# A macaron layer on eight cores: loads of the combine stage issued three tiles ahead, and the output projection's loads on two queues

## The chip, the cores and the metric

One Trainium2 chip, all 8 cores. Each core computes one of the 8 batch entries (2048 tokens x 1024 features, float32) with the same program, and no data passes between cores. The metric is the device time of the slowest core in microseconds.

## The reference, cut to what matters

The layer is half a feed-forward block, attention, and half a feed-forward block again, each on a layer norm of its input. In the feed-forward block every group of 32 tokens is dispatched: each of 128 experts (32 experts x 4 sets) takes the one token of the group with the largest logit, works on it, and its result is added back to that token.

```python
def _L0_ffn_ref(x, controller, f1, bias, f2):
    grouped = x.reshape(B, g, t, d)                      # t = 32
    logits = jnp.einsum('bgtd,des->bgtes', grouped, controller)
    logits = logits + tie
    perm = (logits == jnp.max(logits, axis=-3, keepdims=True))
    dispatched = jnp.einsum('bgtd,bgtes->bgesd', grouped, perm)
    inner = relu(jnp.einsum('bgesd,desf->bgesf', dispatched, f1) + bias)
    intermediate = jnp.einsum('bgesf,esfd->bgesd', inner, f2)
    return jnp.einsum('bgesd,bgtes->bgtd', intermediate, perm)

x = x + 0.5 * _L0_ffn_ref(_layernorm(x), ...)
x = x + _L0_attn_ref(_layernorm(x), ...)   # 16 heads, relative positions, projection by Wo
x = x + 0.5 * _L0_ffn_ref(_layernorm(x), ...)
```

## The kernel before, in words

There is no scheduler. A small builder (class `Bld`) collects one list of instructions for each engine: PE (`tensor`), DVE (`vector`), ACT (`scalar`), POOL (`gpsimd`, GpSimd) and SP (`sync`). Each engine works through its list in order. `b.wait(engine, semaphore, value)` puts a wait into a list, and everything behind it on that engine waits too. `b.dma` (L61) issues a transfer from SP's or GpSimd's list; SP and GpSimd have a DMA queue each (in the profile q1, hardware_dynamic, and q0, software_dynamic), and both are served by the same 16 DMA engines. All SBUF buffers are stretches of one tensor `SCR`, so the profile calls nearly every tile `SCR`.

The program runs in stages, one behind the other:

1. `emit_ln` (layer norm of 2048 tokens), then `emit_ffn`: permutation matrices (L290 to L339), dispatch (L451 to L482), the experts (L519, L575, L605). The result of the experts goes to HBM, to `itb`, in 128 KB pieces by GpSimd.
2. The **combine stage** at the end of `emit_ffn`, L650 to L726. It goes over 16 tiles `t` of 128 tokens. For each, `load_rhs` (L658) loads 4 pieces of `itb`, each 128 x 1024 floats, 512 KB, two from SP and two from GpSimd; `load_xt` (L673) loads the residual tile of `x` or `xs`, 512 KB, from SP. PE multiplies with the permutation (8 matmuls of 128x128x512 at L700; each float32 matmul stands in the trace as two records, so 16 per tile), DVE does `0.5 * P1 + x` in one instruction (L713), and SP stores the tile (L722, 512 KB). PE may not write `P1` again before DVE has read it (L696). There are two buffers for `itb` (`RHS2` and 4096 columns behind it) and two for the residual (`XT`), used in turn.
3. `emit_ln`, then `emit_attn`: 8 pairs of heads, 32 iterations each. Then the **output projection**, L1049 to L1113: eight loads of `aofm` (the attention's result, 1 MB each) and eight of `wot` (512 KB each), then 16 tiles with 16 matmuls of 128x128x512 (L1081) and two additions on DVE (L1093, L1101).
4. `emit_ln` and `emit_ffn` again, with a second combine stage. Its stores go to `out` and end the program.

SP's list in the combine stage is what sets its order. Before the loads of tile t+1 stand these two waits, for PE's work on tile t-1 (which read the `itb` buffer that is filled next) and for the store of tile t-1 (which reads the residual buffer that is filled next):

```python
                    if t >= 1:
                        b.wait("sync", "pe", pesc_hist[t - 1])
                        b.wait("sync", "so", st_hist[t - 1])
                        b.wait("gpsimd", "pe", pesc_hist[t - 1])
                    pre_rhs.append(load_rhs(t + 1, (t + 1) % 2))
                    pre_xt.append(load_xt(t + 1, (t + 1) % 2))
```

`barrier(eng)` (L117) makes one engine wait for everything that was issued so far, by one wait for each semaphore. It stands ahead of each layer norm and ahead of the projection's loads. `DS` (8192 columns from `HBASE + 8192`) holds the dispatched tokens for the experts; in the combine stage nothing reads it.

Of the kernel before, what the change touches and what calls it, by code (L numbers as in the profile page):

```python
# [16 lines left out]
NT = 16  # L17
# [47 lines left out]
def build_nc():  # L65
# [24 lines left out]
    aofm = nc.dram_tensor("aofm", [DM, S], F32).ap()  # L90
# [4 lines left out]
    with ExitStack() as stack:  # L95
        SCR = stack.enter_context(nc.sbuf_tensor("SCR", [128, SCRW], F32))
# [7 lines left out]
        b = Bld(nc, stack)  # L104
        for s_ in ("ld", "sx", "so", "fla", "flb", "fba", "fbb", "fbc", "fbd",
                   "gm", "qwa", "qwb", "qwc", "gra", "grb", "grc",
                   "iwa", "iwb", "rha", "rhb", "xta", "xtb", "aow",
                   "hw", "hr", "lxa", "lxb", "lxc", "lxd", "rga", "rgb",
                   "pe", "ac", "ve"):
            b.sem(s_)  # L110
        DMA_SEMS = ("ld", "sx", "so", "fla", "flb", "fba", "fbb", "fbc", "fbd",
                    "qwa", "qwb", "qwc",
                    "gra", "grb", "grc", "iwa", "iwb", "rha", "rhb",
                    "xta", "xtb", "aow", "hw", "hr", "lxa", "lxb", "lxc", "lxd",
                    "rga", "rgb")

        def barrier(eng):  # L117
            for s_ in DMA_SEMS + ("gm", "pe", "ac", "ve"):
                b.wait(eng, s_, b.cnt[s_])

        def scr(lo, hi, p0=0, p1=128):
            return SCR[p0:p1, lo:hi]
# [140 lines left out]
        def emit_ffn(src_hbm, dst_hbm, h_ve):  # L263
# [11 lines left out]
            DS = HBASE + 8192  # L275
            RHS2 = TAIL
# [9 lines left out]
            for t in range(NT):  # L286
                b.wait("tensor", "ve", b.cnt["ve"])
                for m in range(8):
                    b.op("tensor",
                         lambda e, t=t, m=m: e.matmul(  # L290
                             P1[:, 128 * m:128 * (m + 1)],
                             scr(HBASE + 1024 * t + 128 * m,
                                 HBASE + 1024 * t + 128 * (m + 1)),
                             IDENT[:, :], start=True, stop=True,
                             is_transpose=True),
# [143 lines left out]
            for gh in range(2):  # L439
                for grp in range(2):  # L440
                    for ti in range(8):
                        t = 8 * gh + ti
# [212 lines left out]
            b.wait("gpsimd", "ve", b.cnt["ve"])  # L655
            b.wait("tensor", "ve", b.cnt["ve"])

            def load_rhs(t, slot):  # L658
                lasts = [0, 0]
                for a in range(4):  # L660
                    g = 4 * t + a
                    src = AP(itb.tensor, g * DM, [[NG * DM, 128], [1, DM]])
                    eng = "sync" if a % 2 == 0 else "gpsimd"
                    sem = ("rha" if slot == 0 else "rhb") if a % 2 == 0 \
                        else ("rga" if slot == 0 else "rgb")
                    lasts[a % 2] = b.dma(eng,
                                         SCR[:, RHS2 + 4096 * slot + 1024 * a:
                                             RHS2 + 4096 * slot
                                             + 1024 * (a + 1)],
                                         src, sem)  # L670
                return lasts

            def load_xt(t, slot):  # L673
# [2 lines left out]
                             src_hbm[128 * t:128 * (t + 1), :],  # L676
                             "xta" if slot == 0 else "xtb")

            pre_rhs = [load_rhs(0, 0)]
            pre_xt = [load_xt(0, 0)]  # L680
            pesc_hist = [0] * NT
            vres_hist = [0] * NT
            st_hist = [0] * NT
            st_last = None
            for t in range(NT):
                if t + 1 < NT:
                    if t >= 1:
                        b.wait("sync", "pe", pesc_hist[t - 1])
                        b.wait("sync", "so", st_hist[t - 1])
                        b.wait("gpsimd", "pe", pesc_hist[t - 1])  # L690
                    pre_rhs.append(load_rhs(t + 1, (t + 1) % 2))
                    pre_xt.append(load_xt(t + 1, (t + 1) % 2))
                b.wait("tensor", "rha" if t % 2 == 0 else "rhb", pre_rhs[t][0])
                b.wait("tensor", "rga" if t % 2 == 0 else "rgb", pre_rhs[t][1])
                if t >= 1:
                    b.wait("tensor", "ve", vres_hist[t - 1])  # L696
                for bk in range(2):
                    for a in range(4):
                        b.op("tensor",
                             lambda e, t=t, a=a, bk=bk: e.matmul(  # L700
                                 P1[:, 512 * bk:512 * (bk + 1)],
                                 scr(PRMP + 512 * t + 128 * a,
                                     PRMP + 512 * t + 128 * (a + 1)),
                                 SCR[:, RHS2 + 4096 * (t % 2) + 1024 * a + 512 * bk:
                                     RHS2 + 4096 * (t % 2) + 1024 * a
                                     + 512 * (bk + 1)],
                                 start=(a == 0), stop=(a == 3)),
                             inc="pe")
# [19 lines left out]
        def emit_attn(src_hbm, dst_hbm, hfm_ve):  # L728
# [320 lines left out]
            AOF = XA  # L1049
            XTO = HBASE + 8192  # L1050
            barrier("sync")
            ldw = None
            for m in range(8):
                b.dma("sync", SCR[:, AOF + 2048 * m:AOF + 2048 * (m + 1)],
                      aofm[128 * m:128 * (m + 1), :], "sx")
            for m in range(8):
                ldw = b.dma("sync",
                            SCR[:, HBASE + 1024 * m:HBASE + 1024 * (m + 1)],
                            wot[128 * m:128 * (m + 1), :], "sx")
            b.wait("tensor", "sx", ldw)  # L1060
            b.wait("tensor", "ac", b.cnt["ac"])
            st_last = None
            xt_pre = [b.dma("sync", SCR[:, XTO:XTO + 1024],
# [157 lines left out]
```

How the kernel before makes its waits and increments, by code:

```python
    def wait(self, eng, semname, val):  # L45
        if val is None or val <= 0:
            return
        s = self.sems[semname]
        self.th[eng].append(lambda e, s=s, v=val: e.wait_ge(s, v))
# [1 line left out]
    def op(self, eng, fn, inc=None, n=1):  # L51
        if inc is None:
            self.th[eng].append(fn)
            return None
        self.cnt[inc] += n
        s = self.sems[inc]
        self.th[eng].append(lambda e, fn=fn, s=s, n=n: fn(e).then_inc(s, n))
        return self.cnt[inc]
```

## Time and profile before

| What | Value |
|---|---|
| two timed runs | 9095.19 and 9497.57 us, median 9296.38 us |
| the profiled execution | 8977.86 us |
| its span, from the first to the last instruction of the slowest core | 8975.5 us (the 8 cores: 8934.5 to 8975.5 us) |
| busy share: PE, DVE, ACT, POOL | 86%, 20%, 19%, 6% |
| mean granted clock of PE, as a share of full speed | 0.870 to 0.873 on the 8 cores |
| first combine stage | 1486.2 to 1717.7 us |
| output projection, from its first load to its last tile | 6945.7 to 7288.6 us |
| second combine stage | 8751.5 us to the end |

The times of the profile are microseconds from the start of the span of core 2, the slowest. PE is the matmul engine, PEld its weight loads, SPq the issuing of transfers by SP. "Idle before, releaser" is how long an engine stood still before an instruction and what ended that. The DMA share is the mean busy share of the core's 16 DMA engines; GB/s is what they moved.

### The profile page before, as it was taken

How to read it: one execution, taken by the hardware profiler on the slowest of the kernel's cores; microseconds unless marked ns; L12 is line 12 of the kernel's file. 1: busy time of each engine (PE TensorE's matmuls, PEld its weight loads, DVE VectorE, ACT ScalarE, POOL GpSimd, SP SyncE). 2: the span in 40 equal slices, each digit the busy share in tenths (PEclk: the TensorE clock that was granted, in tenths of full speed). 3: DMA queues.
4: the chain of work that ended last, by engine and by line, in shares of the span. 5: the costliest groups of instructions: out<-in, count | busy, mean ns of one | idle time of the engine just before them, and what ended most of it. 6: DMA issues, size and time to landing. Idle time of an engine off the chain costs nothing.

```text
span 8975.5 us, 109129 instructions; the slowest of 8 cores (8934.5 to 8975.5 us)
## 1 busy us (share of the span) xinstructions
PE 7715.6 (86%) x44416; PEld 5238.7 (58%) x44416; DVE 1750.6 (20%) x3535; ACT 1706.7 (19%) x1511; POOL 573.8 (6%) x1096
## 2 busy tenths in 40 slices
PE   3888887489899899899999999899998757888885
PEld 3664563247757657567577577477477336456542
DVE  3221120202202212112112122022022133112110
ACT  0112212002212212112122122122122000221220
POOL 0001101000000000000000000000000000110110
PEclk7678769789999999999999999999899875986788
DMA  2124325514314324224134144044143220431336
GB/s 81 55 60 133 83 56 167 187 41 153 136 57 155 110 78 158 87 103 157 63 126 155 41 147 158 32 157 143 46 153 135 96 87 0 115 106 54 88 107 225
DMA packets 342583, 962.91 MB, mean 107 GB/s; under 512 B 38096, under 2 KB 198096, under 8 KB 275280
## 3 DMA queue, kind: packets, MB, share of 16 engines
q1 hardware_dynamic: 263248, 578.38, 18.8%
q0 software_dynamic: 78848, 377.56, 12.7%
q8 instruction: 364, 5.96, 0.3%
q14 instruction: 123, 1.01, 0.0%
HBM read 561.65 MB, written 394.13 MB: 106 GB/s over the span
## 4 chain that ended last, share of the span: by engine, by line
PE 82%; DMA 7%; DVE 6%; issue 3%; ACT 2%; SPq 0%; DVEq 0%; ACTq 0%; POOLq 0%; POOL 0%
PE P L934 12%; PE P L970 12%; PE P L866 11%; PE P L785 10%; PE P L468 10%; PE P L605 8%; PE P L923 6%; PE P L1081 3%; PE P L519 3%; PE P L817 3%; DMA itb<-SCR 2%; PE P L700 2%; DMA SCR<-itb 2%; PE P L306 1%; DVE SCR L985 1%
## 5 line engine op out<-in xcount | busy, mean ns | idle before, releaser
L970 PEld LDWEIGHTS P<-SCR 128*128 128x128 f32 x8192 | 999.9, 203 | 251.5 <-issue 251.5
L970 PE MATMUL P<-SCR 128*128 128x128 f32 x8192 | 1047.9, 290 | 65.8 <-ACT SCR L954 65.8
L866 PE MATMUL P<-SCR 64*128 64x512 f32 (+1 forms) x2560 | 1067.5, 565 | 35.6 <-ACT SCR L881 35.6
L934 PE MATMUL P<-SCR 64*128 64x128 f32 x8192 | 1076.6, 283 | 0.0
L605 PE MATMUL P<-SCR 128*32 128x512 f32 x2048 | 904.5, 592 | 149.3 <-DVE SCR L544 121.4
L934 PEld LDWEIGHTS P<-SCR 64*128 64x128 f32 x8192 | 976.9, 192 | 88.6 <-issue 88.6
L954 ACT ACTIVATE SCR<-SCR 128x1024 f32<-128x1024 f32 x512 | 541.2, 1057 | 2314.1 <-DVE SCR L945 2300.2
L620 ACT ACTIVATE SCR<-P 32x1024 f32<-32x1024 f32 x512 | 516.4, 1013 | 2331.9 <-PE P L605 1885.4
L785 PE MATMUL P<-SCR 128*64 128x512 f32 x2048 | 898.0, 602 | 63.2 <-DMA SCR<-wvt 63.2
L468 PE MATMUL P<-SCR 128*128 128x64 f32 x4096 | 877.5, 417 | 60.4 <-DVE SCR L461 60.4
L468 PEld LDWEIGHTS P<-SCR 128*128 128x128 f32 x4096 | 867.4, 329 | 83.0 <-issue 83.0
L945 DVE COPY SCR<-P 128x1024 f32<-128x1024 f32 x512 | 627.2, 1225 | 1239.0 <-PE P L934 1233.7
L866 PEld LDWEIGHTS P<-SCR 64*128 64x128 f32 x2560 | 451.5, 200 | 467.7 <-issue 466.7
L785 PEld LDWEIGHTS P<-SCR 128*64 128x64 f32 x2048 | 284.1, 139 | 671.8 <-issue 671.8
L923 PE MATMUL P<-IDENT,SCR 128*128 128x128 f32 x4096 | 552.6, 279 | 135.4 <-DVE SCR L985 135.4
L605 PEld LDWEIGHTS P<-SCR 128*32 128x32 f32 x2048 | 210.4, 109 | 763.8 <-issue 763.2
L881 ACT ACTIVATE SCR<-P 128x2175 f32<-128x2175 f32 x256 | 507.8, 1984 | 726.8 <-PE P L866 718.7
L923 PEld LDWEIGHTS P<-IDENT,SCR 128*128 128x128 f32 x4096 | 461.8, 143 | 189.3 <-issue 189.3
L61 POOL DMA_DIRECT2D itb<-SCR x512 | 252.1, 492 | 3036.8 <-ACT SCR L620 2719.3
L700 PE MATMUL P<-SCR 128*128 128x512 f32 x512 | 265.1, 678 | 197.0 <-DMA SCR<-itb 176.9
L61 POOL DMA_DIRECT2D SCR<-qsl x256 | 142.1, 555 | 4051.7 <-PE P L934 2304.5
L985 DVE COPY SCR<-P 128x128 f32<-128x128 f32 x256 | 74.6, 291 | 1661.7 <-PE P L970 1661.7
(61 smaller groups left out, 3634.7 us busy)
## 6 DMA issues: line engine op xcount, KB each, us to landing
qsl<-SCR SPq DMA_DIRECT2D x256, 1087.5 KB, 4.1
SCR<-qsl POOLq DMA_DIRECT2D x256, 1024.0 KB, 5.3
SCR<-f2r SPq DMA_DIRECT2D x512, 128.0 KB, 2.4
SCR<-f1r SPq DMA_DIRECT2D x128, 512.0 KB, 4.3
itb<-SCR POOLq DMA_DIRECT2D x512, 128.0 KB, 2.9
SCR<-itb POOLq DMA_DIRECT2D x64, 512.0 KB, 7.2
SCR<-itb SPq DMA_DIRECT2D x64, 512.0 KB, 6.2
xs<-SCR SPq DMA_DIRECT2D x32, 512.0 KB, 4.7
```

The costliest lines, as they stand in the source:

```text
L468: lambda e, hb=hb, m=m, a=a, grp=grp: e.matmul(P0[:, 256 * m + 64 * a: 256 * m + 64 * (a + 1)], scr(hb + 128 * m, hb + 128 * (m + 1)), scr ...
L605: fo=F2S[slot]: e.matmul(P0[0:32, pb + 512 * bk: pb + 512 * (bk + 1)], SCR[0:128, INT + 128 * e4: INT + 128 * e4 + 32], scr(fo + 512 * bk, ...
L620: lambda e, its2=its2, pb=pb: e.activation(scr(ITS2 + 1024 * its2, ITS2 + 1024 * its2 + 1024, 0, 32), P0[0:32, pb:pb + 1024], AF.Copy, sca ...
L700: lambda e, t=t, a=a, bk=bk: e.matmul(P1[:, 512 * bk:512 * (bk + 1)], scr(PRMP + 512 * t + 128 * a, PRMP + 512 * t + 128 * (a + 1)), SCR[: ...
L785: lambda e, wof=wof, hh=hh, nb=nb, m=m: e.matmul(P0[0:64, 512 * nb:512 * (nb + 1)], scr(WSL + 1024 * wof + 128 * m + 64 * hh, WSL + 1024 * ...
L866: lambda e, h=h, q=q, o=o, wd=wd, w0=w0: e.matmul(P0[:, o:o + wd], SCR[0:64, QF + 2048 * h + 128 * q: QF + 2048 * h + 128 * (q + 1)], SCR[ ...
L881: lambda e, i=i: e.activation(SCR[:, sqr_off(i):sqr_off(i) + QW], P0[:, 0:QW], AF.Copy, scale=1.0),
L923: lambda e, i=i, kc=kc, j=j, PS=PS: e.matmul(PS[:, 128 * j:128 * (j + 1)], SCR[:, SPOS + 2048 * (i % 3) + 128 * kc: SPOS + 2048 * (i % 3) ...
L934: lambda e, h=h, q=q, kc=kc, j=j, PS=PS: e.matmul(PS[:, 128 * j:128 * (j + 1)], SCR[0:64, KF + 2048 * h + 128 * kc: KF + 2048 * h + 128 * ...
L945: lambda e, hf=hf, PS=PS: e.tensor_copy(SCR[:, ET + 1024 * hf: ET + 1024 * (hf + 1)], PS[:, 0:1024]),
L954: lambda e, hf=hf: e.activation(SCR[:, ET + 1024 * hf: ET + 1024 * (hf + 1)], SCR[:, ET + 1024 * hf: ET + 1024 * (hf + 1)], AF.Exp, scale= ...
L970: lambda e, voff=voff, kc=kc: e.matmul(P2[:, 0:128] if kc % 2 == 0 else P1[:, 0:128], SCR[:, ET + 128 * kc:ET + 128 * (kc + 1)], SCR[:, VS ...
```

## The change

It has two parts. In the combine stage `itb` gets four buffers in place of two (the two new ones lie in `DS`), each with semaphores of its own for SP's and GpSimd's loads. Three tiles are loaded ahead of the loop, and in iteration t tile t+3. The wait for the store of tile t-1 stands behind these loads now and ahead of the residual tile's load alone. In the output projection the loads of `aofm` are issued by GpSimd, behind a barrier of its own, and PE waits for both kinds of load.

```diff
-            def load_rhs(t, slot):
+            RHSS = (RHS2, RHS2 + 4096, DS, DS + 4096)
+            RSEM_S = ("rha", "rhb", "rhc", "rhd")
+            RSEM_G = ("rga", "rgb", "rgc", "rgd")
+
+            def load_rhs(t):
+                slot = t % 4
                 lasts = [0, 0]
                 for a in range(4):
                     g = 4 * t + a
                     src = AP(itb.tensor, g * DM, [[NG * DM, 128], [1, DM]])
                     eng = "sync" if a % 2 == 0 else "gpsimd"
-                    sem = ("rha" if slot == 0 else "rhb") if a % 2 == 0 \
-                        else ("rga" if slot == 0 else "rgb")
+                    sem = RSEM_S[slot] if a % 2 == 0 else RSEM_G[slot]
...
-            pre_rhs = [load_rhs(0, 0)]
+            pre_rhs = [load_rhs(0), load_rhs(1), load_rhs(2)]
             pre_xt = [load_xt(0, 0)]
...
             for t in range(NT):
+                if t + 3 < NT:
+                    if t >= 1:
+                        b.wait("sync", "pe", pesc_hist[t - 1])
+                        b.wait("gpsimd", "pe", pesc_hist[t - 1])
+                    pre_rhs.append(load_rhs(t + 3))
                 if t + 1 < NT:
                     if t >= 1:
-                        b.wait("sync", "pe", pesc_hist[t - 1])
                         b.wait("sync", "so", st_hist[t - 1])
-                        b.wait("gpsimd", "pe", pesc_hist[t - 1])
-                    pre_rhs.append(load_rhs(t + 1, (t + 1) % 2))
                     pre_xt.append(load_xt(t + 1, (t + 1) % 2))
-                b.wait("tensor", "rha" if t % 2 == 0 else "rhb", pre_rhs[t][0])
-                b.wait("tensor", "rga" if t % 2 == 0 else "rgb", pre_rhs[t][1])
+                b.wait("tensor", RSEM_S[t % 4], pre_rhs[t][0])
+                b.wait("tensor", RSEM_G[t % 4], pre_rhs[t][1])
...
             barrier("sync")
+            barrier("gpsimd")
             ldw = None
+            lda = None
             for m in range(8):
-                b.dma("sync", SCR[:, AOF + 2048 * m:AOF + 2048 * (m + 1)],
-                      aofm[128 * m:128 * (m + 1), :], "sx")
+                lda = b.dma("gpsimd",
+                            SCR[:, AOF + 2048 * m:AOF + 2048 * (m + 1)],
+                            aofm[128 * m:128 * (m + 1), :], "gra")
             for m in range(8):
                 ldw = b.dma("sync",
                             SCR[:, HBASE + 1024 * m:HBASE + 1024 * (m + 1)],
                             wot[128 * m:128 * (m + 1), :], "sx")
             b.wait("tensor", "sx", ldw)
+            b.wait("tensor", "gra", lda)
```

How SP's list moves at the start of the first combine stage, before and after. `SCR<-itb` are the loads of `itb`, `SCR<-x` those of the residual, `xs<-SCR` the stores; `so` counts stores, `pe` PE's work, `ve` DVE's. Before:

```order
206 L61 DMA SCR<-itb 128x1024 [waits iwa,iwb,pe,ve]
207 L61 DMA SCR<-itb 128x1024
208 L61 DMA SCR<-x 128x1024
209 L61 DMA SCR<-itb 128x1024 x2
210 L61 DMA SCR<-x 128x1024
211 L61 DMA xs<-SCR 128x1024 [waits ve]
212 L61 DMA SCR<-itb 128x1024 [waits pe,so]
213 L61 DMA SCR<-itb 128x1024
214 L61 DMA SCR<-x 128x1024
215 L61 DMA xs<-SCR 128x1024 [waits ve]
```

After:

```order
206 L61 DMA SCR<-itb 128x1024 [waits iwa,iwb,pe,ve]
207 L61 DMA SCR<-itb 128x1024 x5
208 L61 DMA SCR<-x 128x1024
209 L61 DMA SCR<-itb 128x1024 x2
210 L61 DMA SCR<-x 128x1024
211 L61 DMA xs<-SCR 128x1024 [waits ve]
212 L61 DMA SCR<-itb 128x1024 [waits pe]
213 L61 DMA SCR<-itb 128x1024
214 L61 DMA SCR<-x 128x1024 [waits so]
215 L61 DMA xs<-SCR 128x1024 [waits ve]
```

Six loads of `itb` stand ahead of the first residual in place of two, and the wait for the store has moved from the loads of `itb` to that of the residual. On GpSimd, at the same place, after the change:

```order
8 L61 DMA itb<-SCR 32x1024 [waits ac] x255
9 L61 DMA SCR<-itb 128x1024 [waits pe,ve]
10 L61 DMA SCR<-itb 128x1024 x7
11 L61 DMA SCR<-itb 128x1024 [waits pe]
12 L61 DMA SCR<-itb 128x1024
13 L61 DMA SCR<-itb 128x1024 [waits pe]
```

Eight loads go out there at once; before the change there were four.

## Rows read from the trace of the kernel before

**Rows 1.** The page: chain of the whole span by engine; GpSimd's largest issues.

```profile
PE 82%; DMA 7%; DVE 6%; issue 3%; ACT 2%; SPq 0%; DVEq 0%; ACTq 0%; POOLq 0%; POOL 0%
...
L61 POOL DMA_DIRECT2D SCR<-qsl x256 | 142.1, 555 | 4051.7 <-PE P L934 2304.5
```

**Rows 2.** Chain that ended last, 1460 to 1720 us: start us, us, what.

```profile
by line: PE P L700 31.4%; DMA SCR<-itb 29.4%; DMA xs<-SCR 20.6%; issue 4.5%; DVE SCR L713 4.3%; PE P L605 4.1%; DMA itb<-SCR 1.8%; SPq L61 1.5%; ACT SCR L620 0.8%; PE P L519 0.5%; PE P L575 0.4%; DVE SCR L586 0.3%; SPq L49 0.3%; DVEq L49 0.
...
1511.06 1.24 DVE SCR L713
...
1512.37 6.17 DMA xs<-SCR
...
1705.09 1.24 DVE SCR L713
...
1715.05 2.60 DMA xs<-SCR
```

**Rows 3.** Timeline, 1470 to 1540 us: start us, us, instructions [idle before <-releaser].

```profile
1502.01 8.88 PE L700 MATMUL P<-SCR 128*128 128x512 f32 x16 [23.46 <-DMA SCR<-itb]
...
1512.44 7.10 PE L700 MATMUL P<-SCR 128*128 128x512 f32 x16 [1.55 <-DVE SCR L713]
...
1519.72 1.23 DVE L713 SCALAR_TENSOR_TENSOR SCR<-P,SCR 128x1024 f32<-128x1024 f32 x1 [7.43 <-PE P L700]
```

**Rows 4.** Groups of instructions, the first combine stage, then the second.

```profile
L700 PE MATMUL P<-SCR 128*128 128x512 f32 x256 | 131.2, 672 | 103.8 <-DMA SCR<-itb 91.4 <-DVE SCR L713 12.4
...
L700 PE MATMUL P<-SCR 128*128 128x512 f32 x256 | 133.9, 683 | 93.2 <-DMA SCR<-itb 85.5 <-DVE SCR L713 7.7
```

**Rows 5.** Busy time by stretch: the first combine stage, then the second.

```profile
core 2: us, PE busy (x) PEld busy (x) DVE busy (x) ACT busy (x) POOL busy (x), PEclk, DMA share, GB/s
1486.20:1717.70 231.50, 131.23 (x256) 54.16 (x256) 19.60 (x16) 0.00 (x0) 14.95 (x29) 0.79 0.66 218
8751.50:8975.50 224.00, 133.89 (x256) 54.88 (x256) 19.60 (x16) 0.00 (x0) 15.06 (x29) 0.80 0.68 225
```

**Rows 6.** DMA issues of the first combine stage, median us to landing.

```profile
SCR<-x SPq DMA_DIRECT2D x16, 512.0 KB, 9.7
xs<-SCR SPq DMA_DIRECT2D x16, 512.0 KB, 8.5
```

**Rows 7.** Busy time by stretch of 2 us; columns as in rows 5.

```profile
1488.00:1490.00 2.00, 0.00 (x0) 0.00 (x0) 0.00 (x0) 0.00 (x0) 0.00 (x0) 0.50 0.96 268
1506.00:1508.00 2.00, 2.00 (x6) 0.95 (x5) 0.00 (x0) 0.00 (x0) 0.00 (x0) 1.00 0.01 4
8756.00:8758.00 2.00, 0.00 (x0) 0.00 (x0) 0.00 (x0) 0.00 (x0) 0.00 (x0) 0.50 1.03 420
8762.00:8764.00 2.00, 2.00 (x4) 0.81 (x3) 0.00 (x0) 0.00 (x0) 0.00 (x0) 0.50 0.95 233
```

**Rows 8.** Timeline, 8745 to 8800 us: the second stage's first addition.

```profile
8770.28 1.23 DVE L713 SCALAR_TENSOR_TENSOR SCR<-P,SCR 128x1024 f32<-128x1024 f32 x1 [33.50 <-PE P L700]
```

**Rows 9.** DMA queues from 8754 to 8756 us: packets, MB, share.

```profile
q0 software_dynamic: 211, 0.74, 91.2%
q1 hardware_dynamic: 22, 0.09, 10.9%
```

**Rows 10.** Groups of instructions, 6944 to 7294 us, the output projection.

```profile
L1081 PE MATMUL P<-SCR 128*128 128x512 f32 x512 | 256.5, 666 | 87.1 <-DMA SCR<-wot 43.9 <-DVE SCR L1101 43.2
```

**Rows 11.** Timeline of SP, 6925 to 6990 us.

```profile
6945.74 5.39 SPq L61 DMA_DIRECT2D SCR<-aofm  x8
```

**Rows 12.** Busy time by stretch, the projection's loads; columns as in rows 5.

```profile
6946.00:6948.00 2.00, 0.00 (x0) 0.00 (x0) 0.00 (x0) 0.00 (x0) 0.00 (x0) 0.50 0.16 25
6976.00:6984.00 8.00, 0.00 (x0) 0.00 (x0) 0.00 (x0) 0.00 (x0) 0.00 (x0) 0.50 1.03 415
```

**Rows 13.** Chain that ended last, 8740 to 8980 us: the longest store.

```profile
8896.18 11.26 DMA out<-SCR
```

**Rows 14.** DMA issues, 1488.2 to 1488.3 us: the first residual tile.

```profile
SCR<-x SPq DMA_DIRECT2D x1, 512.0 KB, 14.8
```

More of the change, by code:

```diff
@@ L107, in build_nc @@
                    "iwa", "iwb", "rha", "rhb", "xta", "xtb", "aow",
-                   "hw", "hr", "lxa", "lxb", "lxc", "lxd", "rga", "rgb",
+                   "hw", "hr", "lxa", "lxb", "lxc", "lxd",
+                   "rga", "rgb", "rgc", "rgd", "rhc", "rhd",
                    "pe", "ac", "ve"):
@@ L114, in build_nc @@
                     "xta", "xtb", "aow", "hw", "hr", "lxa", "lxb", "lxc", "lxd",
-                    "rga", "rgb")
+                    "rga", "rgb", "rgc", "rgd", "rhc", "rhd")
         def barrier(eng):
@@ L663, in load_rhs @@
                     eng = "sync" if a % 2 == 0 else "gpsimd"
-                    sem = ("rha" if slot == 0 else "rhb") if a % 2 == 0 \
-                        else ("rga" if slot == 0 else "rgb")
+                    sem = RSEM_S[slot] if a % 2 == 0 else RSEM_G[slot]
                     lasts[a % 2] = b.dma(eng,
-                                         SCR[:, RHS2 + 4096 * slot + 1024 * a:
-                                             RHS2 + 4096 * slot
-                                             + 1024 * (a + 1)],
+                                         SCR[:, RHSS[slot] + 1024 * a:
+                                             RHSS[slot] + 1024 * (a + 1)],
                                          src, sem)
@@ L703, in emit_ffn @@
                                      PRMP + 512 * t + 128 * (a + 1)),
-                                 SCR[:, RHS2 + 4096 * (t % 2) + 1024 * a + 512 * bk:
-                                     RHS2 + 4096 * (t % 2) + 1024 * a
+                                 SCR[:, RHSS[t % 4] + 1024 * a + 512 * bk:
+                                     RHSS[t % 4] + 1024 * a
                                      + 512 * (bk + 1)],
```

## The prediction, made before the changed kernel was run

> **What bounds the kernel now.** The page comes first: PE leads the chain of work that ended last with 82%, and DMA has 7% of it [rows 1]. So a change to the order of transfers can win only in the few stretches where that chain is not on PE. The chain by time shows where these are. I read it for the first combine stage, from 1486.2 us (SP's first load of `itb`) to 1717.7 us (its last store has landed), 231.5 us. In a window around it PE's L700 has 31.4% of the chain, loads of `itb` 29.4% and stores of `xs` 20.6%. The pieces repeat one pattern seven times: DVE 1.24 us, a store of 6 to 8.5, SP's issue, a load of `itb` of 8 to 10, PE 8.5 to 10, DVE. From the DVE piece at 1511.06 to the one at 1705.09 are 194.0 us for 14 tiles: 27.7 us for two, 13.9 for one [rows 2]. The second combine stage, from 8751.5 us to the end of the span (224.0 us), has the same pattern.
>
> Why two tiles: in the timeline of this stage every second tile starts 1.55 us after the last, with only DVE's add between them [rows 3], and before the other PE waits for `itb`, 91.4 us in all [rows 4]. SP waits for the store of tile t-1 before it may issue the loads of tile t+1, though the `itb` loads write another buffer than the store reads. What ends last there is the chain store, load, PE. No engine is full: PE is busy for 131.2 of 231.5 us [rows 4], the 16 DMA engines for 66% of it at 218 GB/s. While they are busy they thus move 218 / 0.66 = 330 GB/s, in the second stage 225 / 0.68 = 331 [rows 5].
>
> **The change, part by part.** (1) The load of tile t+3 replaces that of t+1, in four buffers, and the wait for the store moves behind it, so that it holds up only the residual tile. Bytes and instructions stay. PE's wait for `itb` (91.4 and 85.5 us, [rows 4]) goes. What is late next is the slowest of three paces:
>
> - PE and DVE: with `itb` there, a tile takes 7.10 us of L700, 1.23 us of DVE and the gaps: 1519.72 - 1511.06 = 8.66 us [rows 2, 3]. That is at the upper level of PE's clock. In a long wait the granted clock reads 0.50, as do the first microseconds of the work behind it; the slice at 1506 us reads 1.00 again [rows 7]. Such a tile takes 8.9 us, not 7.1 [rows 3]. With gaps of 1.55 us every tile should be of the short kind.
> - DMA: a tile moves four pieces of `itb`, one residual and one store, six times 512 KB or 3.146 MB, 9.5 us at 331 GB/s. But more bytes come before the first tile ends (7.86 MB, below); 42.5 MB are left for 15 tiles, 8.6 us each.
> - The chain store(t-1), residual(t+1), DVE(t+1), once in two tiles. The two take 8.5 and 9.7 us to landing in the median [rows 6]; with 1.24 for DVE and about 0.8 for issues that is 20.2 us, 10.1 per tile. I take less: today the residual is issued right behind 2.1 MB of `itb` on both queues ((2.1 + 0.5) / 0.331 = 7.9 us, the rest is a fixed 1.8); after the change it comes some 8 us behind SP's half of them and finds GpSimd's next 1 MB beside it, (1.0 + 0.5) / 0.331 + 1.8 = 6.5 us. 8.5 + 6.5 + 2 = 17 us, 8.5 per tile, as long as the queues drain.
>
> Ends: 8.66 and 10.1 us per tile. I take 9.2: each of the three alone would allow 8.66, but they lie within 0.2 us of each other and will meet in turn.
>
> (2) The start. GpSimd issues eight loads at once, SP six, the first residual, two more, the second residual. Until the first residual has landed, 15 pieces or 7.86 MB have to come, 7.86 / 0.331 = 23.7 us; with about 1 us to begin, the first DVE add starts at 25. Today it starts 1511.06 - 1486.2 = 24.9 us after the stage's start [rows 2], and in the second stage 8770.28 - 8751.5 = 18.8 us [rows 8]. The queues say the same: in a slice in which both have work GpSimd's holds 91.2% of the engines and SP's 10.9% [rows 9], so SP's half of tile 0 lands after 4.19 + 1.05 MB, 15.8 us, and PE's 8.9 us then end at 25 too. The start costs 0 us in the first stage and 6 in the second; both are in the figure 25.
>
> (3) The end stays: DVE 1.24 and the last store 2.60 us [rows 2], about 4.
>
> One stage: 25 + 15 x 9.2 + 4 = 167 us. It saves 231.5 - 167 = 64.5 and 224 - 167 = 57 us, together 121.
>
> From the DMA side: 50.3 MB / 0.331 = 152 us, so 167 asks for engines that are 91% busy, against 66% now. The Trainium skill ("DMA: Bandwidth & Descriptors", Specifications) gives about 358 GB/s as one core's share of the memory that two cores use. Slices here stand on both sides of it, 420 GB/s at a share of 1.03 and 268 at 0.96 [rows 7], and the mean over a stage, 331, decides. By the page's figure a tile needs 3.146 / 0.358 = 8.8 us and the stage 25 + 132 + 4 = 161 us, an estimate that saves 12 us more in all.
>
> (4) The output projection. `aofm` (8.4 MB) moves to GpSimd's queue, `wot` (4.2 MB) stays on SP's. PE waits there for 43.9 us [rows 10]. SP spends 5.39 us on issuing `aofm` ahead of `wot` [rows 11], but the engines are full meanwhile: a share of 0.97 to 1.03 in the four slices of 8 us from 6952 us, at 333, 316, 354 and 415 GB/s, the last of them in [rows 12]. The wait is bytes, and they stay the same. GpSimd issues a load of 1 MB in 0.555 us [rows 1], eight in 4.4, hidden under 36 us of transfer, and its 38 semaphore waits run beside SP's. Value 0. Ends: 2 us gained (from 6946 to 6948 us the share is only 0.16, [rows 12]), or 12.6 MB at 268 instead of 354 GB/s, 11 us lost. The four new semaphores add four waits of 0.05 us to each of SP's three later barriers, 0.6 us, which I leave out.
>
> The Trainium skill has a rule that speaks against this part ("DMA: Bandwidth & Descriptors", Issuing engines are not separate DMA queues): several issuers save only the time of issuing. By it at most SP's 5.4 us could come back; by the rows nothing does, since the issuing lies under the transfer.
>
> **Sum.** The profiled execution took 8977.86 us (the span of 8975.5 and 2.4 around it); less 121 that is 8857. The two timed runs are 9095.19 and 9497.57, median 9296.38: 1.3% and 5.8% over the profiled one. The change touches 5% of the time and won't alter what separates the runs. I forecast on the lower timed run, since the profiled one stands near it: 9095 - 121 = 8974 us.
>
> **Rivals.**
> - R1, the transfers slow down. With all eight cores at 90% DMA the rate could be that of the weakest full slices, about 270 GB/s (268 at 1488 us, 233 at 8762 us, [rows 7]): 50.3 / 0.27 = 186 us, with 6 for start and end 192. It saves 39.5 + 32 = 71.5 us: 9024 us. Against it stand the means of both stages.
> - R2, slower: the chain of store and residual becomes the bound. The deep loads keep both queues full, GpSimd's pieces go ahead, and store and residual stand behind them. Its price: the longest store, 11.26 us [rows 13], and the residual of the first burst, 14.8 us to landing [rows 14], with 1.24 and 0.7 are 28.0 us for two tiles: 25 + 15 x 14.0 + 4 = 239 us, 8 + 15 = 23 us lost, 9118 us. It decides from 25.8 us for store plus residual (27.7 less 1.9). The 91 against 11% speak for it; against it, that 3.1 MB per tile empty in 9.5 us and can't keep the queues full while the chain takes 14.
> - R3, the change doesn't do what it says, because PE's clock stays at the lower level: L700 then takes 2 x 7.1 = 14.2 us, a tile 15.8, the stage 25 + 237 + 4 = 266, 34 + 42 = 76 us lost, 9171 us. Against it: the tile behind a gap of 1.55 us runs in 7.10 us [rows 3].
>
> **How the numbers follow.** Forecast (paces from 8.66 to 10.1, 137 to 94 us saved): 0.62, its own range 8958 to 9001. R1 0.22, R2 0.09, R3 0.02; 0.05 for part 4 losing 10 us or more. These cases differ less than the two timed runs do, so the range has to hold the base too: from 8977.86 - 137 = 8840 to 9296.38 - 121 = 9175, rounded to 9180. The effect I forecast is 1.3 to 1.5%. No case gains 2% (180 us), which is about what a measurement of this kernel can tell from no change; only the spread between runs could show it: 0.2 for faster by over 2%, 0.05 for slower (R2 or R3 with such a spread), 0.75 within.
>
> **What would show it.** Right: DVE adds 8.7 to 10.1 us apart after the first; PE's wait for `itb` in a stage left at the first tile's alone; a granted clock above 0.95 in place of 0.79 [rows 5]; a DMA share near 0.9; the projection's wait still 42 to 55 us. Wrong: DVE waits for the residual's DMA in most tiles (R2), the share is over 0.95 at under 290 GB/s (R1), the clock stays low (R3), or a stage takes more than 185 us.

## The result, and the profile after

Over 19 executions the changed kernel took 9096.43 us in the median (8869.12 to 9674.68), the kernel before 9163.27 us over 18 (8970.54 to 9658.62). The ratio of the two is 0.9905, with a 95% interval of 0.9863 to 0.9947: 85 us less (48 to 123 on 8970 us), within 2%. The clock of one die (cores 0 to 3, or 4 to 7), sometimes of both, is lower in many executions of either kernel, which is why the times spread so far; the ratio is formed from the executions without this, the stage times and the medians of run 9 from the dies without it. The profiled execution of the changed kernel took 8878.12 us, with a span of 8876.1 us on core 3; before, it was 8977.86 with 8975.5 on core 2.

The page's chain by engine, after (before: [rows 1]):

```profile
PE 83%; DMA 6%; DVE 6%; issue 3%; ACT 1%; SPq 0%; DVEq 0%; POOL 0%; ACTq 0%; POOLq 0%
```

Both combine stages by stretch on the slowest core, to be held against [rows 5]. The second and third rows cut the first stage in two, just behind the start of the tenth addition that follows the first:

```profile
core 3: us, PE busy (x) PEld busy (x) DVE busy (x) ACT busy (x) POOL busy (x), PEclk, DMA share, GB/s
1488.60:1666.20 177.60, 123.38 (x256) 50.95 (x256) 19.60 (x16) 0.00 (x0) 14.93 (x29) 0.89 0.87 284
1517.90:1617.70 99.80, 77.36 (x160) 31.84 (x160) 13.41 (x11) 0.00 (x0) 10.47 (x20) 0.93 0.95 311
1617.70:1666.20 48.50, 36.93 (x80) 15.37 (x80) 6.18 (x6) 0.00 (x0) 1.05 (x2) 0.96 0.65 218
8697.40:8876.10 178.70, 122.73 (x256) 50.72 (x256) 19.60 (x16) 0.00 (x0) 14.92 (x29) 0.89 0.85 282
```

The first stage takes 177.6 us in place of 231.5, the second 178.7 in place of 224.0. That is 54 + 45 = 99 us, as much as the span of the slowest core lost (8975.5 - 8876.1 = 99.4), though these are two different cores. The DMA share rose from 0.66 to 0.87. The two stretches show it isn't even: 0.95 at 311 GB/s in the middle, 0.65 in the last 48.5 us.

The groups of L706 (L700 before) and L719 (L713 before), first stage, then second, against [rows 4]:

```profile
L706 PE MATMUL P<-SCR 128*128 128x512 f32 x256 | 123.4, 638 | 57.7 <-DVE SCR L719 34.6 <-DMA SCR<-itb 23.1
...
L719 DVE SCALAR_TENSOR_TENSOR SCR<-P,SCR 128x1024 f32<-128x1024 f32 x16 | 19.6, 1225 | 170.2 <-PE P L706 88.0 <-DMA SCR<-x 82.2
...
L706 PE MATMUL P<-SCR 128*128 128x512 f32 x256 | 122.7, 636 | 59.1 <-DVE SCR L719 37.3 <-DMA SCR<-itb 21.8
...
L719 DVE SCALAR_TENSOR_TENSOR SCR<-P,SCR 128x1024 f32<-128x1024 f32 x16 | 19.6, 1225 | 170.9 <-DMA SCR<-xs 97.7 <-PE P L706 73.2
```

PE's wait for `itb` fell from 91.4 and 85.5 us to 23.1 and 21.8, which is the first tile's alone; on all eight cores and in both stages PE waits for `itb` at that one tile. In its place DVE waits for the residual tile, 82.2 and 97.7 us (`SCR<-x`, `SCR<-xs`), where before it waited for PE only. The chain by time tells when:

```profile
1494.86 22.98 DMA SCR<-x
...
1517.93 1.24 DVE SCR L719
...
1539.44 9.36 DMA xs<-SCR
...
1548.88 8.59 DMA SCR<-x
...
1557.57 1.24 DVE SCR L719
...
1569.21 9.98 DMA xs<-SCR
1579.26 8.11 DMA SCR<-x
...
1654.99 7.12 PE P L706 x16
...
1663.57 2.63 DMA xs<-SCR
```

It starts with the first residual, which lands 23 us after its issue. In the middle the chain runs from a store (9.4 us) to a residual's load (8.6) to DVE; the residual comes last in 5 of the 16 tiles, the first one included (4 to 9 on the eight cores and in both stages). At the end it is on PE alone; the last four additions are 8.65 us apart. DMA issues of the first stage, against [rows 6]:

```profile
SCR<-itb SPq DMA_DIRECT2D x32, 512.0 KB, 10.8
...
SCR<-x SPq DMA_DIRECT2D x16, 512.0 KB, 7.5
xs<-SCR SPq DMA_DIRECT2D x16, 512.0 KB, 8.6
```

The residual's median fell from 9.7 to 7.5 us, the store's stayed at 8.6. The projection's wait, against 43.9 us in [rows 10]:

```profile
6932.66 17.34 PE L1091 MATMUL P<-SCR 128*128 128x512 f32 x32 [44.89 <-DMA SCR<-aofm]
```

One core is a small sample of a stage. Worked out on all eight cores from the starts of DVE's additions, this is the median (and the range) of the time from SP's first load of `itb` to the first addition, the pace between additions, and the stage to its last store's landing (3.9 us after the last addition starts):

| Kernel | first addition, us | pace, us | first stage, us | second stage, us |
|---|---|---|---|---|
| before | 21.2 / 19.0 | 13.4 / 13.4 | 226.5 (218.0 to 231.4) | 225.1 (219.7 to 230.9) |
| after | 26.6 / 26.5 | 9.8 / 9.7 | 178.8 (172.2 to 182.6) | 177.6 (167.8 to 179.7) |

So the change is worth 47.7 + 47.5 = 95 us in the median core. Core 2's 231.5 us, the base of the prediction, was the longest first stage of the eight. Core by core the span doesn't follow the stages as closely as the sum of 99 us suggests: core 3 lost 88 us of span and 96 us in the stages, core 2 lost 124 and 113. PE's clock in the other stages differs from core to core (PE's 512 records of the projection took 234.8 to 257.1 us in these two traces).

### The profile page after: what moved, and what is told of

It is laid out like the page before. It is cut to its first block, busy times and chain, and to the rows that moved or that the text cites. A ratio compares the mean times of both kernels' runs of the same rounds, so it can differ in the third digit from the quotient of the medians.

```text
span 8876.1 us, 109172 instructions; the slowest of 8 cores (8827.9 to 8876.1 us)
## 1 busy us (share of the span) xinstructions
PE 7699.9 (87%) x44416; PEld 5235.4 (59%) x44416; DVE 1751.6 (20%) x3535; ACT 1706.5 (19%) x1511; POOL 575.5 (6%) x1104
## 3 DMA queue, kind: packets, MB, share of 16 engines
q0 software_dynamic: 80000, 385.95, 13.4%
## 4 chain that ended last, share of the span: by engine, by line
PE 83%; DMA 6%; DVE 6%; issue 3%; ACT 1%; SPq 0%; DVEq 0%; POOL 0%; ACTq 0%; POOLq 0%
PE P L940 12%; PE P L976 12%; PE P L872 12%; PE P L791 10%; PE P L469 10%; PE P L606 8%; PE P L929 6%; PE P L1091 3%; PE P L520 3%; PE P L823 3%; DMA itb<-SCR 2%; PE P L706 1%; PE P L307 1%; DMA SCR<-xs 1%; DVE SCR L991 1%
## 5 line engine op out<-in xcount | busy, mean ns | idle before, releaser
L483 DVE COPY SCR<-P 128x512 f32<-128x512 f32 x256 | 262.4, 1025 | 702.7 <-PE P L469 702.7
```

## The experiments

Each ran with a profile; the stages are read in the same way as in the table above. The expectations of runs 1 and 2 set the order of the issues (O) against the depth of the prefetch (D). Those of the later runs name three theories of what bounds the middle of the stage: the chain of waits in SP's list (S), the late residual (R or C), and bandwidth (B).

**1. The order alone.** The kernel before, with the wait for the store behind the loads of `itb`.

```diff
                         b.wait("sync", "pe", pesc_hist[t - 1])
-                        b.wait("sync", "so", st_hist[t - 1])
                         b.wait("gpsimd", "pe", pesc_hist[t - 1])
                     pre_rhs.append(load_rhs(t + 1, (t + 1) % 2))
+                    if t >= 1:
+                        b.wait("sync", "so", st_hist[t - 1])
                     pre_xt.append(load_xt(t + 1, (t + 1) % 2))
```

> The kernel before with the order alone: the store's wait stands behind the loads of itb of tile t+1, two buffers as before. Theory O (the order is the gain): the loads of tile t+1 now start when PE has done tile t-1 and no longer a store later, so the pace between additions of DVE falls from 13.9 us to that of the changed kernel, 9.6 to 9.7, and both combine stages come within 5 us of 178 us. Theory D (the depth is the gain): the 2.1 MB of itb and the 0.5 MB store ahead of them need (2.6 / 0.33) + 1.8 = 9.7 us from PE's end of tile t-1, while PE wants them 1.5 us after; PE waits for itb in every tile, the pace is 10.5 to 11.5 us and a stage takes 185 to 200 us.

Measured on cores 0 to 3: pace 11.1 and 11.3 us, stages of 191.8 and 193.4 us. PE still waits for `itb` (core 2, first stage):

```profile
L701 PE MATMUL P<-SCR 128*128 128x512 f32 x256 | 128.8, 661 | 62.7 <-DMA SCR<-itb 54.8 <-DVE SCR L714 7.9
```

The order gives 35 and 32 us of the 48 per stage. D's numbers came (10.5 to 11.5 us, 185 to 200 us), but not its claim that the depth is the gain.

**2. The depth alone.** The changed kernel, with the wait for the store back in front of the loads of tile t+3.

```diff
                         b.wait("sync", "pe", pesc_hist[t - 1])
+                        b.wait("sync", "so", st_hist[t - 1])
                         b.wait("gpsimd", "pe", pesc_hist[t - 1])
                     pre_rhs.append(load_rhs(t + 3))
```

> The changed kernel with its four buffers and three tiles ahead, but SP's wait for the store of tile t-1 put back in front of the loads of itb (tile t+3). Theory O: the old order brings back the old pace on SP's half, a stage over 210 us. Theory D: PE has three tiles in hand, so a later start of the load costs PE nothing; but the residual of tile t+1 now stands directly behind 1 MB of itb and lands some 3 us later, pace 9.7 to 10.5 us, a stage of 178 to 192 us.

Measured on cores 0 to 3: pace 10.9 and 11.0 us, stages of 195.2 and 194.3 us, both over D's range (9.7 to 10.5 us, 178 to 192 us) and far under O's 210 us. On core 2 PE waits for `itb` at the first tile only; DVE waits for the residual:

```profile
L707 PE MATMUL P<-SCR 128*128 128x512 f32 x256 | 131.6, 673 | 72.7 <-DVE SCR L720 47.3 <-DMA SCR<-itb 25.5
...
L720 DVE SCALAR_TENSOR_TENSOR SCR<-P,SCR 128x1024 f32<-128x1024 f32 x16 | 19.6, 1225 | 193.4 <-DMA SCR<-x 123.4 <-PE P L707 69.9
```

Depth alone gives 31 us of the 48 per stage. Each half of the change gives about two thirds of the whole; they do not add. That is because both draw on the same idle time of the DMA engines, I argue; no run shows it by itself.

**3. The projection alone.** The kernel before with the second part of the change.

```diff
+            barrier("gpsimd")
...
-                b.dma("sync", SCR[:, AOF + 2048 * m:AOF + 2048 * (m + 1)],
-                      aofm[128 * m:128 * (m + 1), :], "sx")
+                lda = b.dma("gpsimd",
+                            SCR[:, AOF + 2048 * m:AOF + 2048 * (m + 1)],
+                            aofm[128 * m:128 * (m + 1), :], "gra")
```

> The kernel before with the change of the output projection alone. By the prediction its value is 0 (from 2 us gained to 11 lost): PE's wait for the loads stays 42 to 46 us, the combine stages stay 231 and 224 us, the span 8960 to 8990 us. A rival (the two queues help each other, 5.4 us of SP's issuing come back) says a wait of 38 to 39 us.

PE's wait was 44.2 us on core 3 (43.9 before on core 2), the stages 226.4 and 227.1 us, the span 8963.1 us. By these numbers the value is 0, as predicted. But core 2's 43.9 us was the longest wait of the eight cores before (37.8 to 43.9, median 40.9). With the loads on two queues the median of the eight is 44.1 us in this run and 43.9 in the changed kernel, and run 1, which leaves the projection as it was, has 42.7 on cores 0 to 3. So this part of the change gained nothing, and may have cost 1 to 3 us.

```profile
L1085 PE MATMUL P<-SCR 128*128 128x512 f32 x512 | 234.6, 618 | 87.4 <-DMA SCR<-aofm 44.2 <-DVE SCR L1105 43.2
```

**4. Four buffers for the residual tile.** SP waits for the store of tile t-3, on a semaphore of each buffer.

```diff
                 if t + 1 < NT:
-                    if t >= 1:
-                        b.wait("sync", "so", st_hist[t - 1])
-                    pre_xt.append(load_xt(t + 1, (t + 1) % 2))
+                    if t + 1 >= 4:
+                        b.wait("sync", STSEM[(t + 1) % 4], st_hist[t + 1 - 4])
+                    pre_xt.append(load_xt(t + 1, (t + 1) % 4))
```

> The changed kernel with four buffers for the residual tile and a semaphore for each buffer's store; the residual is still loaded one tile ahead, behind the loads of itb, but SP now waits for the store of tile t-3 in place of t-1. Theory S (what bounds the middle of the stage is SP itself, which stands in the wait for store t-1, 8.6 to 10 us to landing, before it can issue store t): the wait goes, additions come 8.7 to 9.2 us apart, a stage takes 163 to 171 us. Theory B (bandwidth: the DMA engines are 95% busy there at 311 GB/s, 3.146 MB / 0.327 = 9.6 us per tile): the pace in the middle stays 9.4 to 9.7 us and the stage within 4 us of 178. Theory R (the residual comes late because it stands behind 1 MB of itb in SP's queue): as S, since the residual is asked for earlier as well.

Pace 10.0 and 9.7 us, stages of 181.8 and 176.4 us: no gain. SP's timeline of core 5 shows that the wait did go; the residual is issued right behind `itb` now:

```profile
1566.59 1.20 SPq L61 DMA_DIRECT2D SCR<-itb  x2
1567.88 0.52 SPq L61 DMA_DIRECT2D SCR<-x  x1
1576.42 0.32 SPq L61 DMA_DIRECT2D xs<-SCR  x1
```

But it takes longer to land: from 1520 to 1600 us the median of core 5 is 17.3 us in place of 8.1 (14.1 to 17.3 on the eight cores in place of 7.5 to 9.4). And the engines move what they moved before, 310 GB/s at a share of 0.97 (core 3):

```profile
SCR<-x SPq DMA_DIRECT2D x7, 512.0 KB, 17.3
```

```profile
1523.80:1640.00 116.20, 91.80 (x192) 38.11 (x192) 14.68 (x12) 0.00 (x0) 11.51 (x22) 0.93 0.97 310
```

A request that is made earlier, but behind the same loads of `itb`, only stands longer in the queue. S falls, and so does R as far as the time of the request goes. What this run doesn't try is a residual that goes ahead of the `itb` loads, or more than one tile ahead.

**5. Fewer bytes.** From tile 4 on one of the four pieces of `itb` is not loaded, and PE reads what lay there. The result of these tiles leaves that part out.

```diff
                 for a in range(4):
+                    if a == 3 and t >= 4:
+                        continue
                     g = 4 * t + a
```

> The changed kernel, but one of the four pieces of itb (a = 3, 512 KB, from GpSimd) is not loaded from tile 4 on; PE still does all its matmuls and reads what lay there. A tile then moves 2.6 MB in place of 3.1. Theory B (bandwidth bounds the middle of the stage): 2.62 MB / 0.327 = 8.0 us is under PE's 8.65, so the additions come 8.7 to 9.0 us apart and a stage takes 29 + 131 + 4 = 164 us, 162 to 170. Theory C (a chain of latencies of store and residual, which does not depend on bytes of itb): the pace stays at 9.4 or more, the stage over 172 us.

Pace 8.8 and 8.8 us, stages of 162.2 and 161.4 us. The 6.3 MB that were left out of each stage are worth 16 us of it, and DVE waits for a residual once, at the start (core 5, first stage; us, times, mean us):

```profile
DVE SCR L721 <- PE P L708: 112.8, 15, 8.9
DVE SCR L721 <- DMA SCR<-x: 41.2, 1, 41.2
```

C, whose latencies don't depend on the bytes, would have kept 9.4 us and falls. B fits: with 2.6 MB per tile PE sets the pace. But a chain of store and residual that grows with the bytes queued ahead of it fits as well: the residual landed in 4.9 to 6.5 us here.

B has one gap. In the changed kernel PE waits for `itb` at no tile but the first, on any core. So the lead of three tiles is never drawn down, and the bytes that fill the engines in the middle are bytes that PE needs only later. A stage with the first addition at 26.5 us and every residual in time would take 26.5 + 15 x 8.65 + 4 = 160 us, an estimate from the rows above, and its 50.3 MB need 152 us at 331 GB/s. The run that could tell, with SP's residual ahead of its loads of tile t+3, was not made.

**6. The start's order.** SP issues the first residual behind tile 0.

```diff
-            pre_rhs = [load_rhs(0), load_rhs(1), load_rhs(2)]
+            pre_rhs = [load_rhs(0)]
             pre_xt = [load_xt(0, 0)]
+            pre_rhs += [load_rhs(1), load_rhs(2)]
```

> The changed kernel with one line moved: SP issues the first residual tile right behind the loads of tile 0 and ahead of those of tiles 1 and 2. GpSimd's eight loads still go first. The first addition should come when PE is done, (4.2 + 1.0) / 0.33 + 9 = 25 us after the stage's start in place of 29. Theory B: what follows stays bound by bytes, and the gain shows at the end, where PE had three tiles in hand: a stage of 172 to 175 us in place of 178. The rival (the start is hidden, since the end is set by the total of bytes): the stage stays 177 to 179 us.

First addition at 22.8 and 21.9 us, 4 to 5 earlier, but a pace of 10.1 and 9.8, and stages of 178.8 and 174.9 us (178.8 and 177.6 without it). The rival was right in the first stage, and in the second the difference, 2.7 us, is smaller than the spread of the cores.

**7. The start held back.** As 6, and GpSimd waits for SP's half of tile 0.

```diff
             pre_xt = [load_xt(0, 0)]
+            b.wait("gpsimd", "rha", pre_rhs[0][0])
             pre_rhs += [load_rhs(1), load_rhs(2)]
```

> As the run with the start's order, and GpSimd also waits for SP's half of tile 0 before it issues tiles 1 to 3. Then 3.7 MB or less stand ahead of the first addition: PE starts 8 to 11 us after the stage's start, the first addition comes at 17 to 20 us, near the 18.8 us of the kernel before. Theory B: bytes bound the rest, 50.3 MB / 0.33 + 5 to 8 us, a stage of 158 to 165 us. If PE's three tiles in hand are needed to ride over uneven transfers, the pace in the middle rises to over 10 us and the stage stays above 170 us.

First addition at 18.1 and 18.5 us, 8 earlier; pace 10.2 and 10.1; stages of 176.4 and 173.1 us. The expected 158 to 165 us did not come. Core 2, first stage:

```profile
1500.00:1600.00 100.00, 72.65 (x148) 30.06 (x149) 11.02 (x9) 0.00 (x0) 12.54 (x24) 0.91 0.98 314
1600.00:1660.00 60.00, 47.09 (x104) 19.59 (x103) 7.35 (x6) 0.00 (x0) 3.15 (x6) 0.97 0.78 262
```

The engines are full until 1600 us and not after, as without the hold. What stays is the tail in which the last tiles' `itb` already lies in SBUF and PE works it off at 8.65 us each; an earlier start doesn't shorten it, since the loads keep their lead. That this tail is the reason is argued from these rows; run 10, with a lead shorter by a tile, does not show it clearly. Where the last 10 us above the bytes' time go stays open; late residuals, as under run 5, are the other candidate.

**8. Early loads for the projection.** In the last pair of heads SP issues `wot` and the first three parts of `aofm`, one behind each of eleven stores, into space that the last pair no longer reads. Five loads of `aofm` stay at the head of the projection.

```diff
                         emit_wr(i + DEPTH); emit_rd(i + DEPTH)
+                        early_load(i - 4)
```

> The changed kernel, with the eight loads of wot and those of aofm rows 0 to 2 moved from the head of the output projection into the last pair of attention, one behind each store of SP (into space that held the normalized tokens, which the last pair no longer reads); five loads of aofm stay. By the prediction's reading the wait at the head is bytes (12.6 MB): 5.2 MB are left, 5.2 / 0.35 + 3 = 18 us, so PE's wait falls from 44 to 17 to 20 us, the span by 24 to 27 us, and attention stays as long as it was. If the wait were issuing, 5 of 16 loads left would leave about the same share; if the loads in attention stood in the way of its own transfers, the last pair would grow by more than 5 us.

Core 2, before PE's first matmul of the projection; the changed kernel waits 44.2 us there on this core:

```profile
L1107 PE MATMUL P<-SCR 128*128 128x512 f32 x512 | 234.8, 618 | 67.5 <-DVE SCR L1127 43.2 <-DMA SCR<-aofm 24.3
```

24.3 us in place of 44.2, 20 us won (24 to 27 expected). From the start of L823 in the last pair to GpSimd's issue of the last `aofm` store it takes 519.9 us in both kernels, so the early loads cost nothing there. It is bytes, as the prediction had it. The fixed part is larger than the 3 us that I had put: the five loads and the first two residual tiles (6.3 MB) move at 315 GB/s in the mean, at a share of 0.84.

```profile
6887.00:6907.00 20.00, 0.17 (x1) 0.20 (x2) 0.00 (x0) 0.00 (x0) 2.65 (x5) 0.50 0.84 315
```

**9. Both additions,** the edits of 7 and 8 in one kernel, timed beside the changed kernel and once more alone.

> The changed kernel with the held start (SP: first residual behind tile 0; GpSimd waits for SP's half of tile 0) and the early loads of wot and of three parts of aofm. The parts should add: 2 to 5 us from each combine stage and 20 from the projection's wait, as each gave alone; 25 to 28 us under the changed kernel in the profile (spans near 8840), a ratio to the kernel before of 0.985 to 0.989 in the same rounds, 0.003 under the changed kernel's. If they only trade places with each other or the early loads cost elsewhere, the ratio equals the changed kernel's.

> The changed kernel as it is, timed in the same rounds as the run before, so that both have the same base: a ratio of 0.988 to 0.992 to the kernel before (the first measurement gave 0.9905), the combine stages at 172 to 183 us on all eight cores.

> The same kernel as in the run with both additions (held start and early projection loads), timed again, since only one of its six executions there was free of disturbance. In that run the slower core of each undisturbed die took 8840 us in the median, that of the kernel before 8980, that of the changed kernel 8872. If these hold, the ratio to the kernel before is 0.984 to 0.986; if the additions gain nothing in the whole program, it is the changed kernel's 0.990.

The changed kernel again has 0.9899 (0.9844 to 0.9954), its stages 180.9 and 175.2 us in the median, but 168.9 to 186.6 us over the eight cores where 172 to 183 was expected. With both additions the stages are 178.3 and 175.1 us, so the held start gained nothing worth the name in this run; the projection's wait is 22.7 us (core 0) against 44.0. There is no ratio of its own for it. Of each die with a mean clock over 0.868 I take the slowest core; the medians are 8969 us before, 8872 changed and 8840 with both (10, 10 and 7 dies), in the second run 8975 before and 8854 with both (8 and 7 dies). So the kernel with both additions is 32 us under the changed kernel where both were timed, and 129 and 121 us under the kernel before, ratios of 0.986 and 0.987 (0.985 to 0.989, then 0.984 to 0.986 expected); these differences have no interval. The span of the profiled execution, 8854.9 us, is 15 us over the 8840 expected. The parts did add, but nearly all of it is the projection's wait.

**10. Two tiles ahead.** Three buffers, the start as in 6.

```diff
-                if t + 3 < NT:
+                if t + 2 < NT:
```

> The changed kernel with three buffers and itb loaded two tiles ahead, the first residual behind tile 0. Theory B: two tiles in hand keep the DMA engines as full as three (95% in the middle), and the tail in which PE works off what lies ready is one tile shorter: first addition at 21 to 24 us, a stage of 170 to 178 us, no slower than the changed kernel. If the third tile is what keeps the engines full, the pace rises towards the 11.1 us of one tile ahead, a stage of 180 to 190 us.

On cores 4 to 7: first addition at 22.9 and 21.1 us, pace 10.1 and 9.9, stages of 178.9 and 172.4 us (170 to 178 expected). Within the spread of these four cores, 168.2 to 181.4 us, two tiles in hand are as good as three.

## Why the prediction was right or wrong, point by point

The mechanism held: the misplaced wait and the short lead were the cost, and the gain came from the two combine stages. What failed is the base of the forecast ("I forecast on the lower timed run", 9095 - 121 = 8974 us), and, by a smaller amount, the pace of 9.2 us. Set against the median of 9296 us the point stood for a gain of 3.5%; measured are 0.95%, 85 us where the sum said 121.

**What bounds the stage, and what goes: right.** The alternation of store, load and PE was the cost. Runs 1 and 2 show both halves of it, 35 and 31 us of the 48 in the first stage. PE's wait for `itb` went down to the first tile's, and the start and the tail remained.

**The pace, 9.2 us: mis-sized, 9.8.** The term that was mis-sized is the second of the three paces, "42.5 MB are left for 15 tiles, 8.6 us each". It spread the bytes evenly over all tiles. But the lead of three tiles holds to the end: the last tiles load nothing, and theirs is time in which the engines are at 0.65. In the middle each tile moves its full 3.146 MB. At the rate that the engines have while busy, 311 / 0.95 = 327 GB/s, that is 9.6 us, near the 9.5 that the first half of the same bullet gave; at the 311 GB/s that they moved it is 10.1. On core 3 eleven intervals took 109.7 us, 10.0 each, the last four 8.65 each. A mean of bytes over a stage hides that its two ends can't use the engines. The rest, 0.4 us, is about the 5% in which the engines stood idle. The rows on the clock below show what a late residual does to PE: from 1548.17 to 1558.94 and on to 1569.29 us two tiles take 10.8 and 10.4 us in place of 8.65. So two paces that lie close take turns, and a turn costs more than the difference. Whether the bytes or the late residual come first in this is not shown (run 5). The third term, the chain of store and residual, was put at 8.5 with an upper end of 10.1 us. The chain of the changed kernel runs through it, as my rival R2 said. Run 4 shows that requesting the residual earlier behind the same loads doesn't shorten it, run 5 that it goes with fewer bytes.

**The start, 25 us: mis-sized, 26.6 in the median, 29.3 on the slowest core.** PE began 1504.11 - 1488.6 = 15.5 us into the stage (15.8 predicted). The residual, for which I counted 7.86 MB, came when 8.81 MB had moved, at 301 GB/s:

```profile
DMA packets 2410, 8.81 MB, mean 301 GB/s; under 512 B 259, under 2 KB 259, under 8 KB 2410
...
q0 software_dynamic: 1189, 4.35, 49.5%
q1 hardware_dynamic: 1221, 4.47, 44.7%
```

SP's queue had moved 4.47 MB, 8.5 pieces in place of my seven, so pieces that were issued later had overtaken part of it. Runs 6 and 7 show that this term hardly counts for the stage: what is won at the start comes back in the pace.

**The sum, 121 us: 99 in the profiles, 95 in the median core, 85 by the ratio** (48 to 123, so 121 is just inside). Of the 22 us between 121 and 99, 8 are the start (29.3 and 28.7 us on core 3) and 14 the pace (9.62 and 9.72 us there, 0.42 + 0.52 over 9.2, times 15). The check from the DMA side, "engines that are 91% busy", should have warned: they came to 87 and 85%.

**The time, 8974 us: 122 too low.** The median of 9096 lies in the range, but the point does not hold. The step that failed is "I forecast on the lower timed run": two runs that were 4.4% apart can't give a base to 1%. Over 18 executions the kernel before has 9163 us, 68 above the 9095 that I took. Set against the 9296 us that stood beside it, the point also read as a gain of 3.5%, where my own sum gave 1.3%. I should have given the gain as a ratio of that median, 9296 x 0.9865 = 9171. That point would have been 75 us too high instead, but it would have said 1.3%.

**The clock, above 0.95: wrong, 0.89.** I took it that every gap would be 1.55 us. The timeline of PE shows what a gap can do to the tile behind it; the last two rows are of the second stage:

```profile
1548.17 7.11 PE L706 MATMUL P<-SCR 128*128 128x512 f32 x16 [1.55 <-DVE SCR L719]
1558.94 8.80 PE L706 MATMUL P<-SCR 128*128 128x512 f32 x16 [3.66 <-DVE SCR L719]
...
1617.90 8.52 PE L706 MATMUL P<-SCR 128*128 128x512 f32 x16 [2.97 <-DVE SCR L719]
1629.04 7.11 PE L706 MATMUL P<-SCR 128*128 128x512 f32 x16 [2.62 <-DVE SCR L719]
...
8797.04 7.10 PE L706 MATMUL P<-SCR 128*128 128x512 f32 x16 [3.25 <-DVE SCR L719]
...
8826.92 10.18 PE L706 MATMUL P<-SCR 128*128 128x512 f32 x16 [2.99 <-DVE SCR L719]
```

The granted clock reads 1.00 in the tile at 8797.04 us and 0.70 in the one at 8826.92, with 0.50 from 8828 to 8832 us, though its gap was shorter.

**The projection, 0 us: right within its ends** (2 us gained to 11 lost), by the wait of the slowest cores (43.9, 44.9 and 44.2 us) and by run 3, though the medians say 1 to 3 us lost; run 8 shows from the other side that the wait is bytes. The Trainium skill ("DMA: Bandwidth & Descriptors", Issuing engines are not separate DMA queues) says that several issuing engines save only the time of the issuing. Even that, SP's 5.4 us, did not come back here. The Trainium skill's 358 GB/s ("DMA: Bandwidth & Descriptors", Specifications) is stated as a limit, and the mean of 327 GB/s in the busy time stays under it; the estimate that was worked out from it, 8.8 us per tile, came out too fast, since the middle's pace was 10.0.

**The rivals.** R1 (270 GB/s) fell: the rate while busy is 326 to 332 GB/s before and after (284 / 0.87 and 282 / 0.85 after). R2's mechanism is there in part (DVE waited for the residual in 4 to 9 of the 16 tiles of a stage), its price is not. R3 fell, though the clock costs more than I gave it. The chances: within 2% had 0.75, and it is within.

## What to carry to other kernels

When a prefetch removes a wait, work out the middle, where each step moves its full bytes at the rate of the busy engines, and the tail, where the lead is worked off with idle engines, apart; a mean over the stage is too kind. Ahead of a deeper prefetch ask which wait stands in front of which issue: here moving one wait gave two thirds of the gain without any buffer. Once the engines are full, asking earlier behind the same transfers only lengthens the time to landing (run 4), and fewer bytes help (run 5). Then look at what stands ahead of the late transfer: if it is a prefetch whose data nobody waits for, as here, its place in the queue is the next thing to try. And a forecast of 1% needs a base that is known to 1%; give it as a ratio.

## What the runs showed of the hardware that I had not expected

PE's tile of 16 records takes 7.1 us at the upper level of its clock, and 8.5 to 10.2 us where the clock has fallen for a part of it. A gap's length alone doesn't tell which: in both stages of the changed kernel, on all eight cores, the 144 tiles behind gaps under 1.6 us all took 7.1 us, and the 62 behind gaps of 3.5 us and more took 8.5 to 10.2. Of the 50 tiles in between 27 took 7.1 us and 23 took 8.5 or more, one of them behind a gap of only 1.9 us. So a wait of 3 us can cost PE 3 us or 6 (the tiles behind 3.25 and 2.99 us above).

With both queues full, the time to landing is no property of a transfer: the same 512 KB of the residual took 7.5 to 9.4 us in the changed kernel (medians of the eight cores, 1520 to 1600 us), 14.1 to 17.3 us when it was asked for earlier (run 4) and 4.9 to 6.5 us when a sixth of the bytes was gone (run 5). The engines moved nearly the same in all three: 299 to 315, 294 to 307 and 289 to 299 GB/s.
